# Two blocks of a vision transformer on one core: MLPs on flat groups of 384 tokens that pass through HBM, and a reordered embedding loop

## What is computed

```python
h = tokens(x)                                   # patches @ W.T + b, class token, positions
h = h + attn0(norm(h))                          # 64 first tokens query the other 133, projection
h = h + (gelu_tanh(norm(h) @ W0.T + b0) @ W1.T + b1)       # W0 = w_fc * C0, W1 = w_proj * C1
h = h + attn1(norm(h))                          # 12 heads of 64 over the 197 tokens of an image
h = h + ffn(norm(h))                            # integers -8..7: round(clip(x/a)), gelu, clip, round
```

## Time and profile before

| | us |
|---|---|
| median of three runs (2715.95 to 2720.96) | 2718.76 |
| the profiled execution | 2716.97 |
| its span | 2714.9 |

### The profile page before, as it was taken

The page is one execution under the profiler, slowest core; times in us unless marked ns, Lnnn a source line. Parts: engine busy times, 40 slices in busy tenths (PEclk is TensorE's granted clock), DMA queues, the critical chain, the costliest instruction groups (busy, mean ns, idle before and its releaser), DMA issues. The chain is left out here.

```text
span 2714.9 us, 83446 instructions
## 1 busy us (share of the span) xinstructions
PE 2498.4 (92%) x27448; PEld 2120.4 (78%) x27448; DVE 2254.3 (83%) x5864; ACT 2089.7 (77%) x6198; POOL 1232.4 (45%) x1805
## 2 busy tenths in 40 slices
PE   5878886999997999999999999999999999996776
PEld 5767774888885888888888888888888888884554
DVE  6767876777775888888888888888888888887998
ACT  4867895555554888888888888888888888886998
POOL 6867882333331343434343334334433443344664
PEclk9988996999998999999999999999999999997999
DMA  6422330000001333333233333333333333320111
GB/s 202 134 81 84 103 90 1 1 0 0 0 0 37 73 81 68 74 72 80 67 73 75 79 68 70 77 77 70 67 80 74 73 67 80 72 63 14 40 43 46
DMA packets 181704, 173.54 MB, mean 64 GB/s; under 512 B 19063, under 2 KB 180289, under 8 KB 181378
## 3 DMA queue, kind: packets, MB, share of 16 engines
q1 hardware_dynamic: 181634, 172.64, 26.2%
HBM read 46.68 MB, written 9.68 MB: 21 GB/s over the span
## 5 line engine op out<-in xcount | busy, mean ns | idle before, releaser
L1323 POOL TENSOR_TENSOR b_pr<-b_pr,b_rinv 128x394 f32<-128x394 f32 (+1 forms) x768 | 626.5, 843 | 1006.8 <-DVE b_rinv L1281 1006.8
L1218 ACT ACTIVATE b_pr<-b_banks,b_nmx 128x197 f32<-128x197 f32 (+1 forms) x1536 | 625.8, 424 | 27.5 <-DVE b_nmx L1275 25.3
L1189 ACT ACTIVATE b_pt<-b_bank_t 128x394 f16<-128x394 f32 (+1 forms) x768 | 337.8, 494 | 202.7 <-PE b_bank_t L1154 202.5
L1275 DVE TENSOR_REDUCE b_nmx<-b_banks 128x2 f32<-128x394 f32 (+1 forms) x768 | 397.3, 558 | 65.5 <-PE b_banks L1144 57.3
L1246 DVE TENSOR_TENSOR b_pt<-b_bank_t,b_pt 128x394 f16<-128x394 f32 (+1 forms) x768 | 395.9, 556 | 18.2 <-ACT b_pt L1189 18.2
L1128 PE MATMUL b_banks<-b_xt,wqkv 128*128 128x197 f16 x3840 | 374.0, 249 | 4.4 <-DVE b_xt L1246 2.2
L1154 PE MATMUL b_bank_t<-ident,b_pr 128*128 128x128 f32 (+3 forms) x3072 | 341.8, 253 | 3.1 <-DVE b_pt L1246 3.0
L1128 PEld LDWEIGHTS b_banks<-b_xt,wqkv 128*128 128x128 f16 x3840 | 321.0, 98 | 25.5 <-issue 18.8
L1144 PE MATMUL b_banks<-b_kst,b_qst 128*128 128x197 f16 (+1 forms) x3072 | 326.7, 248 | 7.4 <-ACT b_pr L1218 4.9
L1154 PEld LDWEIGHTS b_bank_t<-ident,b_pr 128*128 128x128 f32 (+3 forms) x3072 | 282.1, 142 | 42.9 <-issue 35.4
L1218 ACT ACTIVATION_READ_ACCUMULATOR b_pr<-b_banks,b_nmx 128x1 f32 (+1 forms) x1536 | 315.0, 205 | 0.0
(11 more groups left out here) (206 smaller groups left out, 4665.0 us busy)
## 6 DMA issues: line engine op xcount, KB each, us to landing
b_qst<-b_qk SPq DMA_DIRECT2D x512, 147.8 KB, 2.5
b_kst<-b_qk SPq DMA_DIRECT2D x512, 73.9 KB, 2.3
patches<-in_x SPq DMA_DIRECT2D x64, 588.0 KB, 4.3
out<-z_res SPq DMA_DIRECT2D x32, 192.0 KB
out<-z_res SPq DMA_DIRECT2D x32, 103.5 KB
h<-in_wqkv SPq DMA_DIRECT2D x2, 1152.0 KB, 6.5
h<-in_w SPq DMA_DIRECT2D x2, 576.0 KB, 7.0
h<-in_fc SPq DMA_DIRECT2D x1, 768.0 KB
```

The source lines that it names most:

```text
L1189: return nc.scalar.activation(dst, src, ACT.Copy)
L1218: last = nc.scalar.activation(pr[n % 3][0:ROWS[c], c, e, :], banks[0:ROWS[c], c, e * SEQ:(e + 1) * SEQ], ACT.Exp, bias=nmx[n % 2][0:ROWS[c ...
L1275: v.reduce_max(nmx[n % 2][0:ROWS[c], c, :], banks[0:ROWS[c], c, 0:2 * SEQ].rearrange("p (e t) -> p e t", e=2), AX.X, negate=True).then_inc ...
L1323: last = nc.gpsimd.tensor_tensor(p, p, inv, ALU.mult)
```

## The change

Between the stages the stream now also goes through HBM, as flat rows: `stream` is 12,672 rows (33 groups of 384) of 198 numbers, 192 of the token and its six of statistics. `embed_attend` stores each pair into it. `mlp_0` works on 33 groups of 384 tokens, three full pieces of 128 rows, in a ring of four slots: load, own statistics (a), aggregate (r), own root chain of 14 steps on GpSimd (q), norm (n), and at the end sum (f), new statistics (s), store, and from there the rows of each image back into the tile for the second attention. `attention_1` stores each image's rows. `mlp_1` takes groups too, with a ring of four, one root chain for two groups, a second load of the rows for the last addition, which moves from VectorE to GpSimd (A), two of six roundings moved from ScalarE to VectorE (v2, v5), and the bias as one more product of the down sum in place of GpSimd's addition: split in three bfloat16 parts, picked by a matrix of ones and zeros.

In `embed_attend` the root chain is done once for two pairs on eight columns; the keys' update moves from ScalarE to VectorE as an addition of the norm (u); the statistics at its end (s) go; the down weights come in the other layout, so that turning them on TensorE goes and a column mask replaces it; and all four orders are new. Both MLPs use `rounds`, unrolled by four. The core of the diff:

```diff
-PE_ORDER = "x^^ t^^^ E1 m^^^ s^^ j^^^^ E0'".split()
-ACT_ORDER = ("e^^^^ g^^^^^ h0 u^^^ k^^^ n^^ h1 x^^").split()
-DVE_ORDER = ("x^^ p^^^ f^^^^^ o^^^^ t^^^ a0 s^^^^^ b0 a1 b1 i^^^ r m^^").split()
-POOL_ORDER = ("l00 l01 l02 l10 l11 q1^ q2^ q3^ q4^ q5^ l12 q6^ q7^ q8^ q9^ q10^ "
+PE_ORDER = "E1 t^^^^ x^^^ j^^^^^ m^^^^ s^^^ E0'".split()
+ACT_ORDER = ("h1 k^^^^ n^^^ x^^^ h0' e^^^^ g^^^^^").split()
+DVE_ORDER = ("f^^^^^^ m^^^^ a0 x^^^ p^^^^ u^^^^ o^^^^^ t^^^^ b0 a1 b1 i^^^^ r").split()
+POOL_ORDER = ("l00 l01 l02 l10 l11 l12 q1^ q2^ q3^ q4^ q5^ q6^ q7^ q8^ q9^ q10^ "
              "q11^ q12^ q13^ q14^ q15^").split()
 QKV_PART = 3 * HID // 2
...
+def job(s, p, like):
+    if s == "d":
+        load(s, p, like)
+        return
+    sp.wait_ge(h_done, p + 1)
+    for c in range(2):
+        rows = stream[0:n_img * SEQ, 0:D].rearrange("(i t) d -> t i d", t=SEQ)[c * P:c * P + ROWS[c], bass.ds(2 * p, 2), :]
+        sp.dma_start(rows, h[0:ROWS[c], bass.ds(2 * p, 2), c, :]).then_inc(pair_stored, 16)
+rounds(sp, ["d", STORE], count, job, {"d": {1: load_masks, 3: load_quantised, 5: load_attention(0), 7: load_attention(1),
...
+if b == 0:
+    return
+moment = lambda k: mv[:, :, :, k].rearrange("p b j -> p (b j)")
 if n == 1:
     pool.wait_ge(aggregated, p + 1)
-    last = g.tensor_tensor(var[b][:], mv[b][:, :, 1], eps[:], ALU.add)
+    last = g.tensor_tensor(var[:], moment(1), eps[:], ALU.add)
 else:
...
+elif kind == "u":
+    dve.wait_ge(xn_made, p + 1)
+    for c, rows in ((0, slice(NK1, P)), (1, slice(0, TAIL))):
+        keys = h[rows, bass.ds(2 * p, 2), c, :]
+        last = v.tensor_tensor(keys, keys, xn[b][rows, :, c, :], ALU.add)
+    last.then_inc(keys_added, 1)
...
-def take_turned_weights(n):
-    def take():
-        dve.wait_ge(turned, n + 1)
-        for f in range(2):
-            v.tensor_copy(S["fp"][:, 0, 2 * n + f, :], bank_t[f])
-        if n == 2:
-            v.tensor_copy(S["fc_bias"][:], bank_b)
-        then(v.memset(gate[:, 3:4], 0.0))
-        for f in range(2):
-            last = v.tensor_tensor(S["fp"][:, 1, 2 * n + f, :], bank_t[f], S["fp"][:, 0, 2 * n + f, :], ALU.subtract)
-        last.then_inc(weights_taken, 1)
-    return take
...
+def split_bias():
+    b, rows, picked = S["q2_bias"], S["bias_rows"], S["picked"]
+    then(v.reciprocal(c1b[:], S["q2_scale"][:]))
+    then(v.tensor_tensor(b[:], b[:], c1b[:], ALU.mult))
+    then(v.tensor_copy(rows[:], b[:]))
+    then(v.tensor_tensor(b[:], b[:], rows[:], ALU.subtract))
+    v.tensor_copy(rows[32:64, :], b[32:64, :])
+    then(v.tensor_copy(rows[64:P, :], b[64:P, :]))
+    then(v.tensor_tensor(b[64:P, :], b[64:P, :], rows[64:P, :], ALU.subtract))
+    v.tensor_copy(rows[64:P, :], b[64:P, :])
+    then(v.memset(picked[:], 0.0))
+    for row in (0, 32, 64):
+        last = v.memset(picked[row:row + 1, :], 1.0)
+    then(last)
...
+total = n_img * SEQ
+count = -(-total // GROUP)
+LAST_ROOT = 14
+PE_ORDER = "U^ T D^^".split()
+ACT_ORDER = "g0^ g1^ h0^ g2^ h1^ g3^ h2^ g4^ h3^ g5^ h4^ h5^ c".split()
+DVE_ORDER = "n w0^ w1^ a' w2^ w3^ r' w4^ w5^ x f^^ s^^".split()
+POOL_ORDER = ["B"] + [f"q{n}'" for n in range(1, LAST_ROOT + 1)]
...
+@block.sync
+def _(sp):
+    def load(g):
+        if g >= 4:
+            sp.wait_ge(stored[g % 4], 16 * (g // 4))
+        sp.dma_start(ring[g % 4][:, :, 0:D], group_rows(stream, g, D)).then_inc(loaded[g % 4], 16)
+    sp.wait_ge(zeroed, 1)
+    pads = list(range(total, count * GROUP, P))
+    for at in pads:
+        n = min(P, count * GROUP - at)
+        sp.dma_start(stream[at:at + n, :], zeros[0:n, :]).then_inc(padded, 16)
+    ahead_of_use = min(3, count - 1)
+    for g in range(ahead_of_use):
+        load(g)
+    sp.wait_ge(padded, 16 * len(pads))
+    sp.wait_ge(stats_cleared, 1)
+    image = 0
+    for g in range(count):
+        if g + ahead_of_use < count:
+            load(g + ahead_of_use)
+        while image < n_img and (SEQ * (image + 1) - 1) // GROUP < g:
+            for c in range(2):
+                at = SEQ * image + c * P
+                for k in sorted({at // GROUP, (at + ROWS[c] - 1) // GROUP}):
+                    sp.wait_ge(stored[k % 4], 16 * (k // 4 + 1))
+                sp.dma_start(rows_of_images[0:ROWS[c], image, c, :], stream[at:at + ROWS[c], :]).then_inc(returned, 16)
+            image += 1
+        sp.wait_ge(row_done, g + 1)
+        sp.dma_start(group_rows(stream, g, W), ring[g % 4][:]).then_inc(stored[g % 4], 16)
+    for k in range(max(0, count - 4), count):
+        sp.wait_ge(stored[k % 4], 16 * (k // 4 + 1))
+    for image in range(image, n_img):
+        for c in range(2):
+            at = SEQ * image + c * P
+            sp.dma_start(rows_of_images[0:ROWS[c], image, c, :], stream[at:at + ROWS[c], :]).then_inc(returned, 16)
+    sp.wait_ge(returned, 32 * n_img)
...
+def job(s, p, like):
+    b, slot = like % 2, like % 4
+    if s == "B":
+        pool.wait_ge(xn_made, p + 1)
+        for c in range(TILES):
+            stream_part = ring[slot][:, c, 0:D]
+            last = g.tensor_tensor(stream_part, stream_part, S["fp_bias"][:], ALU.add)
+        last.then_inc(bias_added, 1)
+        return
+    n = int(s[1:])
+    if n == 1:
+        pool.wait_ge(aggregated, p + 1)
+    else:
+        pool.wait_ge(root_step_done, LAST_ROOT * p + n - 1)
+    if n == LAST_ROOT and later(p - 1):
+        pool.wait_ge(xn_made, p - 1)
...
+def job(s, p, like):
+    b, slot, kind = like % 2, like % 4, s[0]
+    x = ring[slot]
+    if kind == "a":
+        dve.wait_ge(loaded[slot], 4 * p + 16 - 4 * slot)
+        v.memset(gate[:, 0:1], 0.0)
+        for c in range(TILES):
+            last = v.bn_stats(st[:, c, :], x[:, c, 0:D])
+        last.then_inc(counted, 1)
+    elif kind == "r":
+        dve.wait_ge(counted, p + 1)
+        v.memset(gate[:, 0:1], 0.0)
+        for c in range(TILES):
+            last = v.bn_aggr(mv[b][:, c, :], st[:, c, :])
+        last.then_inc(aggregated, 1)
+    elif kind == "n":
+        dve.wait_ge(root_step_done, LAST_ROOT * (p + 1))
+        if later(p - 1):
+            dve.wait_ge(turned, p - 1)
+        for c in range(TILES):
+            scalars = [mv[b][:, c, 0:1], rstd[b][:, c:c + 1], ALU.subtract, ALU.mult]
+            v.tensor_scalar(xn[b][:, c, 0:P], x[:, c, 0:P], *scalars)
+            twice = x[:, c, P:D].unsqueeze(1).to_broadcast([P, 2, LO])
+            last = v.tensor_scalar(xn[b][:, c, P:2 * P].rearrange("p (a b) -> p a b", a=2), twice, *scalars)
+        last.then_inc(xn_made, 1)
+    elif kind == "x":
+        dve.wait_ge(xt_hi, p + 1)
+        v.tensor_tensor(xt[b][:, 2, :], bank_x[0][:, 0:GROUP], xt[b][:, 0, :], ALU.subtract)
+        v.tensor_tensor(xt[b][LO:P, 1, :], bank_x[1][LO:P, 0:GROUP], xt[b][LO:P, 1, :], ALU.subtract).then_inc(xt_split, 1)
+    elif kind == "w":
+        f = int(s[1])
+        dve.wait_ge(hid_hi, HC * p + f + 1)
+        v.tensor_tensor(hid[b][:, 1, f, :], act_out[(2 * b + f) % 4][:], hid[b][:, 0, f, :], ALU.subtract).then_inc(hid_split, 1)
+    elif kind == "f":
+        dve.wait_ge(made_y, p + 1)
+        dve.wait_ge(bias_added, p + 1)
+        for c in range(TILES):
+            last = v.tensor_tensor(x[:, c, 0:D], y_part(c), x[:, c, 0:D], ALU.add)
+        last.then_inc(h_done, 1)
+    else:
+        dve.wait_ge(h_done, p + 1)
+        v.memset(gate[:, 1:2], 0.0)
+        for c in range(TILES):
+            last = v.bn_stats(x[:, c, D:W], x[:, c, 0:D])
+        last.then_inc(row_done, 1)
...
+if kind == "o":
+    sp.wait_ge(row_done, img + 1)
+    for c in range(2):
+        rows = stream[0:n_img * SEQ, :].rearrange("(i t) w -> t i w", t=SEQ)[c * P:c * P + ROWS[c], bass.ds(img, 1), :]
+        sp.dma_start(rows, S["rows"][0:ROWS[c], bass.ds(img, 1), c, :]).then_inc(stored, 16)
+    return
...
+LAST_ROOT = 15
+PE_ORDER = "U^ T D^^".split()
+ACT_ORDER = "G0^ R4^^ G1^ G2^ R0^ G3^ R1^ G4^ G5^ R3^".split()
+DVE_ORDER = "c0^ f^^^ c1^ c2^ x v2^ c3^ c4^ n' c5^ r''' v5^ y'".split()
+POOL_ORDER = [f"q{n}'''" for n in range(1, 7)] + ["A^^^"] + [f"q{n}'''" for n in range(7, LAST_ROOT + 1)]
+ON_ACT, ON_DVE = (0, 1, 3, 4), (2, 5)
...
+def load(g):
+    if g >= 4:
+        sp.wait_ge(xn_made, g - 3)
+    sp.dma_start(ring[g % 4][:], group_rows(stream, g, W)).then_inc(loaded[g % 4], 16)
+def load_again(g):
+    if g >= 2:
+        sp.wait_ge(h_done, g - 1)
+    sp.dma_start(again[g % 2][:], group_rows(stream, g, D)).then_inc(reloaded[g % 2], 16)
...
+for g in range(min(4, count)):
+    load(g)
+for g in range(min(2, count)):
+    load_again(g)
+for g in range(4, min(6, count)):
+    load(g)
+sent = [0, 0]
+for g in range(count):
+    if g + 6 < count:
+        load(g + 6)
+    sent[g % 2] += store(g)
+    if g + 2 < count:
+        load_again(g + 2)
...
+if s == "A":
+    pool.wait_ge(scaled, p + 1)
+    pool.wait_ge(reloaded[b], 8 * p + 16 - 8 * b)
+    for part in (slice(0, 2), slice(2, 3)):
+        r = res[b][:, part, :]
+        last = g.tensor_tensor(r, again[b][:, part, :], r, ALU.add)
+    last.then_inc(h_done, 1)
+    return
...
```

(73 more changed lines are left out.)

727 lines of the change are left out of this document (349 added, 378 removed).

## The result

The changed kernel takes 2774.33 us (median of four runs, 2767.15 to 2780.06) against 2719.7 for the kernel before on the same chip: a ratio of 1.0203, 95% interval 1.0183 to 1.0223. Forecast was 2724, range 2680 to 2762. It is slower, and by more than the range allowed.

The account below looks back on a forecast made before the run. GpSimd was taken to bound the embedding loop, TensorE the first MLP and second attention, VectorE the second MLP. Terms -41 + 24 + 3 + 19 = +5 us gave a forecast of 2724 us, range 2680 to 2762.

Parts of the forecast that it names:

- Part 1: Embedding loop: set by GpSimd, whose work the change cuts; the stage was to fall by 41 us (-62 to -17).
- (b): Embedding loop: GpSimd's root chain once for two pairs, 28 rounds of 10.3 us for 11.15, -24 us (-42 to -6).
- (a): Embedding loop: down weights come in the right layout, so their turning goes from three rounds, -25 us.
- (c): Embedding stage, added work: bias split +3, pipeline one round deeper +3, last pair's store +2.5, together +8 us.
- Rival D: Embedding loop: VectorE becomes the bound, its additions meeting GpSimd's splits; -41 becomes -17, whole 2748 us; chance 0.08.
- Part 2: First MLP: the ring's store and load in a row hold rounds at 11.8 us, stage +24 us (-31 to +60).
- Rival A: Both MLPs: the ring's transfers are hidden, rounds of 10.0 and 6.8 us, whole 2647 us; chance 0.12.
- Part 3: Second attention: loop untouched; last store and tables on strided statistics cost +3 us (0 to 6).
- Part 4: Second MLP: A and three queued transfers delay every other round nearly 2 us; 7.5 us each, +19 us (-3 to +36).

Follow-up runs that it names:

- h2: h1 plus six spare matmuls in TensorE's queue of each embedding round, ahead of its wait for o: 2672.6 us, 0.9834 of the kernel before.
- h1: Changed kernel with eight slots in first MLP, A first and r early in second, preparation at the end of embedding rounds: 2687.1 us, ratio 0.9885.
- i1: Changed kernel with only six spare matmuls added ahead of TensorE's wait for o in each embedding round: 2771.5 us, 1.0199 of the kernel before.
- e5: Changed kernel with all of VectorE's preparation of the weights left out, so later numbers are wrong: 2733.1 us, 1.0059 of the kernel before.
- e7: Changed kernel with eight ring slots instead of four in the first MLP, loads five groups ahead: 2722.1 us, 1.0027 of the kernel before.
- f3: Changed kernel with eight slots in first MLP, A first and r early in second, embedding preparation at round ends, bias split spread: 2678.5 us, 0.9865.

## Why the prediction was wrong

**Part 1 failed, with -41 for +8, and in it step (b), rounds of 10.3 in place of 11.15.** In the terms of the sum, for the loop (predicted -46, came -5.8):

- (a) came: the three rounds with turned weights take 63.0 us before and 41.9 after, -21 for -25.
- (b), and the bias split of (c), did not: the other 28 rounds take 11.76 us on the mean before and 12.30 after, +15 for -21. Two things that the step put at nothing are in it, the low level of the clock and VectorE's preparation beside u.

*The clock.* I read the late rounds at a clock of 1.00 in the earlier trace rows and carried that clock into all of the loop. The same view of the kernel before has, for earlier stretches, 0.91 and 0.85, and I didn't use them:

```profile
50.00:150.00 100.00, 80.40 (x916) 70.18 (x914) 73.32 (x247) 74.68 (x140) 80.76 (x191) 0.91 0.42 127
150.00:250.00 100.00, 79.93 (x851) 70.50 (x849) 72.91 (x264) 71.24 (x134) 64.83 (x156) 0.85 0.28 80
```

At full clock the loop fell from 364.9 to 338.6, -26. The prediction, with the 24 us of low level taken out that stand beside the three turnings before (12 us of loop time), asked for 346.2 - 15.4 = 331: 8 us missing. The clock took 27 us before and 48 after, where the prediction has room for 15 without saying so: 32 us, the bulk of the 40 that the loop misses. At full clock step (b) is nearly right: rounds 24 to 30 without a fall take 10.0 to 11.1 us, and without preparation the 28 rounds take 10.93 us before and 10.37 after; as measured, with the low level in them, they take 11.06 and 11.10.

*The preparation.* It cost the loop 22.4 us before and 38.0 after, where the sum takes it as hidden but for the 3 us of the bias split. Of these 15.6 us, 4 are there at full clock (12 before, 16 after) and 12 are low level: 34.1 of 54.6 us stay without it before, 51.2 of 95.6 after. Without the preparation the change still saves only 21 us in the loop, where (a) and (b) say 49.

That the clock is a cause and not a companion is shown by h2 against h1; how much of the 32 us could be had back in the kernel after as it stands isn't shown, since i1 got none.

What stands ahead of a fall is a wait of TensorE in the middle of a round: each of the fifteen falls in the loop after begins inside a wait of 1.0 us or more, or up to 2.2 us behind its end. Their sum doesn't tell how much of the clock is lost: it sank, from 73 us in the loop before to 65, while the low level grew. Before there are twelve falls of 4.6 us on the mean, nine of them of 3.4 us each besides the three at the turnings; its 36 gaps ahead of the token products between 100 and 413 us have 0.86 us on the mean and up to 2.1. After there are fifteen falls of 6.4 us. Why these last longer isn't shown. Eleven of them, with 75 of the 96 us, stand in two places:

- Four falls of 10.2 us each, 41 us, are in rounds 3, 4, 13 and 17, at waits of 2.2 to 5.6 us for VectorE's xs and prs. Preparation steps stand in all four rounds, and in e5 no wait for xs or prs is left.
- Seven falls, 34 us, follow within 4 us a gap ahead of j of 1.4 to 1.55 us, where u holds o. There are eleven such gaps and five smaller ones. At 295.49 u starts, with 2.33 us for both additions; o follows at 297.85, j at 298.83:

```profile
295.49 2.33 DVE L725 TENSOR_TENSOR rows<-rows,xn 64x384 f32<-64x384 f32 x2
...
297.85 0.85 DVE L749 SCALAR_TENSOR_TENSOR o<-bank_o,rinv,o 64x192 f16<-64x192 f32 x2
...
298.83 0.34 PE L537 MATMUL bank_r<-pb_two,ones 128*128 128x192 f16 x1 [1.41 <-DVE o L749]
```

Rival D had this place and price for u (2.0 taken; measured 2.33 in 15 of the 32 pairs, each with GpSimd's splits beside it, 1.74 in one, and 1.12 in 16, of which 14 have no split beside them), but not the clock behind it, and VectorE isn't full: 302 of 386 us. So its +29 for the whole, nearer to the measured +55 than the forecast's +5, comes by another mechanism.

Step (c), a pipeline one round deeper, +3, and the last store, +2.5, is the second term that was wrong, mis-sized by 10 us: from the last pair's first token addition to the end of the stage it is 32.0 us before and 47.3 after. Last pair, before and then after (chain's end on GpSimd, start of n on ScalarE):

```profile
424.41 0.20 POOL L354 TENSOR_TENSOR my<-negated,y 128x4 f32<-128x4 f32 x1
424.79 1.85 ACT L399 ACTIVATE xn<-h,my,y 128x192 f32<-128x192 f32 x4
```

```profile
419.94 0.20 POOL L374 TENSOR_TENSOR a_my<-a_negated,a_rstd 128x8 f32<-128x8 f32 x1
...
429.68 1.86 ACT L424 ACTIVATE xn<-rows,a_my,a_rstd 128x192 f32<-128x192 f32 x4
```

The root is ready at 420.1, for two pairs at once, and n of the last pair starts 9.5 us later: n of the pair before it comes first (421.23), then x, e, g and k of other pairs in ScalarE's written order; before it was 0.2 us. From n to the last addition it is 19.5 us before and 20.2 after. From there to the end of the stage, with the store, it is 4.1 us (449.9 to 454.0) in place of 1.5. The ends of the range don't follow from the terms either: -25, -42 and +8 give -59, not -62, and -25, -6 and +8 give -23, not -17.

**Part 2 was right** by its own mechanism: transfers 5.7 for 5.6, rounds 11.70 for 11.8, and without the ring 10.0 for 10.0. Stage +18 for +24: from the first group's first gelu to the last group's it is 370.5 us for the 375.6 predicted, and the end is 2 us shorter. Rival A's size (-31) would have been -33 by e7. **Part 3** came out at +3. **Part 4** had the pattern, 7.76 for 7.5 (by its own terms, 6.7 and 1.9 more in every other round, 7.65), and the wrong releaser: I queued A and three transfers ahead of r; it is r at the end of VectorE's round that starts the chain too late for n (with r early the rounds go from 7.47 to 6.79), and A inside it adds 0.3. VectorE's own round was 6.7 by the prediction, 6.79 in f3.

## What to carry to other kernels

Read the granted clock over the whole of a loop, not over its quietest rounds: here the loop's length was a fixed number at full clock plus half the time on the low level, and an edit is to be priced on both. A new order need not hide the work that the old one hid (here the preparation, 22.4 us in the path before and 38.0 after), so price that again too. An order that puts TensorE's long products in one piece leaves the short ones bare, so a small job moved onto another engine ahead of them can become a gap, and removing one gap may only move it to the next engine. A ring whose slot must be stored before it is loaded again should have enough slots that no round waits for both transfers; here going from four to eight slots was worth 51 us, nearly the whole loss, which was 55.
